# Routing a mixture of experts in groups of four tiles, and its expert loop written out

## The reference

```python
gu = x @ shared_gate_up_w
shared = _silu(gu[:, :Is]) * gu[:, Is:] @ shared_down_w
shared = shared * jax.nn.sigmoid(x @ shared_gate_w)
probs = jax.nn.softmax((x @ gate_w), axis=-1)
w, idx = jax.lax.top_k(probs, TOP_K)             # TOP_K = 8
w = w / jnp.sum(w, axis=-1, keepdims=True)
pos = ...   # how many earlier rows chose this expert
slot = jnp.minimum(pos, CAPACITY)                # CAPACITY = 128
buf = jnp.zeros((E, CAPACITY + 1, H)).at[e_flat, slot].set(x[tok])
act = _silu(gu_e[..., :I]) * gu_e[..., I:]       # gu_e = buf @ expert_gate_up_w
y = (act @ expert_down_w)[e_flat, slot] * w_flat[:, None]
y = jnp.where((pos < CAPACITY)[:, None], y, 0)
```

## Time and profile before

| | us |
|---|---|
| median of 3 runs (2916.77 to 2929.06) | 2918.77 |
| profiled execution | 2919.06 |
| its span | 2917.2 |
| `route` in it, first part | 1559.6 to 1652.3 |
| `route`, second part | 1652.3 to 1752.5 |
| `experts` | 1753.9 to 1889.3 |

### The profile page before, as it was taken

How to read it: one execution, slowest core, us unless ns; L and a number is a source line. 1 busy time by engine, 2 the same in 40 slices (tenths; PEclk the granted TensorE clock), 3 DMA queues, 4 the chain that set the end, 5 groups by cost and what they waited for, 6 DMA issues and landing times. The chain is left out here.

```text
span 2917.2 us, 69083 instructions
## 1 busy us (share of the span) xinstructions
PE 2553.8 (88%) x24287; PEld 1964.5 (67%) x24301; DVE 1767.3 (61%) x4144; ACT 1308.0 (45%) x3086; POOL 1479.7 (51%) x1701
## 2 busy tenths in 40 slices
PE   5875999999999999997785697859999999997996
PEld 2434878787878787785564455647888888885664
DVE  5654757575757576774565682346666665653663
ACT  3542646464646464653441223325444445442431
POOL 5774757475757475764661125456554445322320
PEclk9997999999999999998995699979999999999996
DMA  4331111111111111110002407553333334210000
GB/s 146 121 126 51 46 35 45 28 45 36 45 28 44 33 45 31 41 33 10 24 4 88 122 0 256 181 167 109 93 84 81 71 85 97 64 41 14 4 4 30
DMA packets 219788, 189.90 MB, mean 65 GB/s; under 512 B 86433, under 2 KB 206899, under 8 KB 219491
## 3 DMA queue, kind: packets, MB, share of 16 engines
q1 hardware_dynamic: 203378, 150.88, 17.4%
q0 software_dynamic: 10624, 30.99, 4.4%
q10 hardware_dynamic: 5488, 3.94, 0.5%
HBM read 151.42 MB, written 34.31 MB: 64 GB/s over the span
## 5 line engine op out<-in xcount | busy, mean ns | idle before, releaser
L840 POOL TENSOR_TENSOR rk<-ss,neg_half 128x32 f32<-128x32 f32 x64 | 347.5, 5430 | 212.1 <-DVE ss L746 212.1
L940 ACT ACTIVATE score<-score,ntop 128x289 f32<-128x289 f32 x256 | 135.4, 530 | 257.7 <-DVE ntop L757 254.9
L1024 PE MATMUL banks<-x_hi,wk_hi 128*128 128x256 f32 x1024 | 219.2, 297 | 32.0 <-DVE kT L740 31.2
L1544 PE MATMUL banks<-rowsT,qk 128*128 128x257 f32 x1024 | 243.1, 380 | 0.9 <-ACT qk L1471 0.9
L1024 PE MATMUL banks<-x_hi,wk_lo 128*128 128x256 f32 x1024 | 211.1, 289 | 0.0
L1024 PE MATMUL banks<-x_lo,wk_hi 128*128 128x256 f32 x1024 | 210.3, 288 | 0.0
L740 DVE COPY kT<-banks 128x512 f32<-128x512 f32 x256 | 176.0, 688 | 52.5 <-PE banks L1024 50.3
L1544 PEld LDWEIGHTS banks<-rowsT,qk 128*128 128x128 f32 x1024 | 189.2, 190 | 27.4 <-ACT qk L1471 1.2
L918 ACT ACTIVATE ksq<-kT 128x512 f32<-128x512 f32 x256 | 161.2, 630 | 85.1 <-DVE kT L740 83.1
L1024 PEld LDWEIGHTS banks<-x_hi,wk_hi 128*128 128x128 f32 x1024 | 163.5, 196 | 35.5 <-DVE kT L740 25.8
L754 DVE CUSTOM_DVE_ANT_0 score<-banks,rkb 128x289 f32<-128x289 f32 x256 | 108.7, 457 | 120.4 <-PE banks L1075 73.6
(11 more groups left out here) (364 smaller groups left out, 6799.0 us busy)
## 6 DMA issues: line engine op xcount, KB each, us to landing
rowsT<-in_ctxT SPq DMA_DIRECT2D x64, 257.0 KB, 2.8
raw<-in_ctx SPq DMA_DIRECT2D x64, 256.0 KB, 2.7
wgu<-in_expert_gu SPq DMA_DIRECT2D x64, 256.0 KB, 3.3
rows<-in_ctx SPq DMA_DIRECT2D x64, 256.0 KB, 3.1
scratch_qT<-qT SPq DMA_DIRECT2D x16, 512.0 KB, 2.6
scratch_kT<-kT SPq DMA_DIRECT2D x16, 512.0 KB, 3.2
q<-scratch_qT SPq DMA_DIRECT2D x64, 128.0 KB
kT<-scratch_kT SPq DMA_DIRECT2D x64, 128.0 KB
```

The source lines that it names most:

```text
L840: nc.gpsimd.tensor_tensor(m.rk[:], m.ss[:], kit.neg_half[:, 0:KF * H], ALU.pow).then_inc(s.rk, 1)
L940: nc.scalar.activation(m.score[:, c, :], m.score[:, c, :], ACT.Exp, bias=m.ntop[:, c:c + 1], accum_out=m.mass[:, c:c + 1]).then_inc(s.p, 1)
L1024: mm = nc.tensor.matmul(key_bank[i % 2][:, a * ROWS:(a + 1) * ROWS], w[:, f, pr * P:(pr + 1) * P], x[:, k, f, :], start=(at == 0), stop=(a ...
L1544: mm = nc.tensor.matmul(score[h][:, c - h * HALF, 0:CTX], m.qk[:, f, j, c * BT:(c + 1) * BT, :].rearrange("p h q -> p (h q)"), m.rowsT[:, ...
```

## The change

1. **Routing in groups of four tiles.** DVE runs over four tiles at once where it can (logit copy, `chosen`, `keep`, `place`, `key` are 256 columns); MAX8 and MATCH_REPLACE8 of the logits stay per tile. Eight normed tiles have buffers of their own, stored without weights (256 words). `before`, `ones` and `chosen` are bf16 (0 and 1 are exact), and the counting is done by matmuls over all earlier tiles' masks.
2. **Weights late.** Logits of all tiles are kept; shift, exponential, mask, sum and scale run once over 1024 columns, and one store in pieces of 64 words puts them beside the rows.
3. **Lists from two half lists.** Keys of rows 0 to 1023 go to partitions 0 to 63 and those of rows 1024 to 2047 to partitions 64 to 127, over 1024 columns. 16 rounds make both lists; the second half's slots are counted from the end, so that the reversing matrix `anti` and two matmuls add both lists into one.
4. **Shared network beside the routing.** Gate and up products are put between the routing steps on PE; POOL's copy of the transposed rows is gone, since ACT writes them in place.
5. **Experts written out.** No loops; the gather takes its numbers from `token` directly and waits for its ring slot. Weights are now the stationary side and the rows move, 128 columns, so that hidden rows come out transposed and their transpose and copy fall away. The routing weight is applied at the output. Fetches of the later experts' weights are spread over 56 of the 64 experts.

The core of the diff:

```diff
-                with sp.Fori(0, NT // 2) as u:
...
-                        sp.dma_start(d.routed_tiles[n], m.routed[:, k, :]).then_inc(stored[k], 16)
...
+                for n in range(NT):
+                    sp.wait_ge(s.xl, n + 1)
+                    sp.dma_start(d.routed_tiles[n][:, 0:D], m.rows[:, n % RT, :]).then_inc(stored[n % RT], 16)
+                    for e in range(n * (E_ // 2 // NT), (n + 1) * (E_ // 2 // NT)):
+                        early.load_one(sp, e, e, early.loaded)
+                sp.wait_ge(s.w, 1)
+                sp.dma_start(d.routed_tiles.rearrange("t p d -> p t d")[:, :, D:ROUTED], share).then_inc(s.weights_out, 16)
...
+                def largest(r):
+                    if r == 0:
+                        dve.wait_ge(s.ring, len(RING))
+                    else:
+                        dve.wait_ge(s.struck, r)
+                    nc.vector.max(m.order[:, 8 * r:8 * r + 8], m.keyT[:]).then_inc(s.order, 1)
...
+                for g, after in ((0, 5), (1, ROUNDS - 11)):
+                    for i in range(GT_):
+                        add(GT_ * g + i)
+                        if i % 2 == 0:
+                            strike(r)
+                            r += 1
+                        else:
+                            largest(r)
+                    for _ in range(after):
+                        strike(r)
+                        r += 1
+                        if r < ROUNDS:
+                            largest(r)
...
+                def inner(n, part):
...
+                    if n > 0:
+                        pe.wait_ge(s.gated if part == 0 else s.up, n)
...
+                for g in range(GN):
+                    for i in range(GT_):
+                        if g == 2 and i == 0:
+                            pe.wait_ge(s.order, ROUNDS)
+                            nc.tensor.transpose(kit.psum(2)[:, 0:P], m.order[:], kit.ident[:]).then_inc(s.order_ps, 1)
+                        if g == 2 and i == 2:
+
+                            pe.wait_ge(s.orderT, 1)
+                            nc.tensor.matmul(kit.psum(3)[:, 0:E_], kit.ident[:], m.orderT[:, 0:E_], start=True, stop=False)
+                            nc.tensor.matmul(kit.psum(3)[:, 0:E_], wm.anti[:], m.orderT[:, E_:2 * E_], start=False, stop=True).then_inc(s.list_ps, 1)
+                        outer(GT_ * g + i)
+                    for n in range(SN * (g + 2), min(SN * (g + 3), SN * GN)):
+                        inner(n, 0)
+                        inner(n, 1)
...
+        def due(e):
+
+            return [i for i in range(TURN) if (7 * i + 3) // 4 == e]
...
+                    for i in due(e):
+                        sp.wait_ge(s.y_ps, i + 1)
+                        weights.load_one(sp, TURN + i, i, late_in[i])
...
-                        nc.gpsimd.tensor_copy(m.index[:, b, :], kept.token[:, bass.ds(e, 1)]).then_inc(s.index, 1)
-                        hold(pool, s.index, e + 1, s.passed)
-                        nc.gpsimd.indirect_dma_start(m.rows[:, b, :], None, d.routed, bass.IndirectOffsetOnAxis(m.index[:, b, :], 0)).then_inc(rows_in[b], 16)
...
+                    if e >= EB:
+                        pool.wait_ge(s.out, e - EB + 1)
+                    nc.gpsimd.indirect_dma_start(m.rows[:, e % EB, :], None, d.routed, bass.IndirectOffsetOnAxis(kept.token[:, e:e + 1], 0)).then_inc(rows_in[e % EB], 16)
...
+                    for part in range(2):
+                        for f in range(FC):
+                            mm = nc.tensor.matmul(kit.psum(2 + e % 4)[:, part * CAP:(part + 1) * CAP], weights.wgu[:, e % TURN, f, part * I_:(part + 1) * I_], m.rowsT[:, e % 2, f, :],
+                                                  start=(f == 0), stop=(f == FC - 1))
                     mm.then_inc(s.gu_ps, 1)
...
+                for e in range(E_):
+                    if e + 2 < E_:
+                        rows_T(e + 2)
+                    if e + 1 < E_:
+                        products(e + 1)
+                    output(e)
```

More of the change, by code:

```diff
@@ L2387, in _, with group, rows @@
-                nc.vector.memset(m.count[:], 0.0).then_inc(s.c_set, 1)
+                def group(g):
+                    return slice(GT_ * g, GT_ * g + GT_)
+                def rows(first, count):
+                    if first >= RT:
+                        dve.wait_ge(s.ring_ps, RING["rows", (first + count - RT) // GT_ - 1, 1] + 1)
+                    for n in range(first, first + count):
+                        if n >= RT:
+                            dve.wait_ge(stored[n % RT], 16 * (n // RT))
+                        norm.rows(m.rows[:, n % RT, :], n).then_inc(s.xl, 1)
@@ L2388, in _ @@
                 norm.ready(dve)
+                nc.vector.memset(m.far_key[:], 0.0).then_inc(s.c_set, 1)
+                rows(0, 8)
                 dve.wait_ge(weights.loaded, weights.count)
[L2390 to L2434, removed]
@@ new lines, in logits @@
+                def logits(g):
+                    pe.wait_ge(s.ring, RING["rows", g, 1] + 1)
+                    if g > 0:
+                        pe.wait_ge(s.logit, g)
+                    for i in range(GT_):
+                        n = GT_ * g + i
+                        for f in range(FC):
+                            mm = nc.tensor.matmul(kit.psum(2)[:, i * (E_ + 1):(i + 1) * (E_ + 1)], m.xlT[:, f, n * P:(n + 1) * P], wm.wg[:, f, :], start=(f == 0), stop=(f == FC - 1))
+                    mm.then_inc(s.lg_ps, 1)
@@ new lines, in _ @@
+                inner(2, 0)
+                rows_T(3, 0)
+                rows_T(3, 1)
+                inner(2, 1)
+                logits(3)
+                places(2)
+                keys_T(1)
+                inner(3, 0)
+                inner(3, 1)
+                places(3)
+                keys_T(2)
+                inner(4, 0)
+                inner(4, 1)
+                keys_T(3)
+                for n in range(5, 8):
+                    inner(n, 0)
+                    inner(n, 1)
@@ new lines, in output @@
+                def output(e):
+                    dve.wait_ge(s.y_ps, e + 1)
+                    if e >= EB:
+                        dve.wait_ge(stored[e % EB], 16 * (e // EB))
+                    nc.vector.tensor_scalar(m.out[:, e % EB, :], kit.psum(6 + e % 2)[:, 0:D], m.rows[:, e % EB, D + e:D + e + 1], None, ALU.mult).then_inc(s.out, 1)
+                hidden(0)
+                for e in range(E_):
+                    if e + 1 < E_:
+                        hidden(e + 1)
+                    output(e)
@@ new lines, in output @@
+                def output(e):
+                    pe.wait_ge(s.hid, e + 1)
+                    if e >= 2:
+                        pe.wait_ge(s.out, e - 1)
+                    nc.tensor.matmul(kit.psum(6 + e % 2)[:, 0:D], m.hidT[:, e % 2, :], weights.wd[:, e % TURN, :], start=True, stop=True).then_inc(s.y_ps, 1)
+                rows_T(0)
+                rows_T(1)
+                products(0)
+                for e in range(E_):
+                    if e + 2 < E_:
+                        rows_T(e + 2)
+                    if e + 1 < E_:
+                        products(e + 1)
+                    output(e)
```

531 lines of the change are left out of this document (271 added, 260 removed).

## The result

| | us | ratio to before (95% interval) |
|---|---|---|
| kernel before, median of 4 runs | 2919.15 | |
| kernel after, median of 4 runs (2817.97 to 2826.43) | 2822.97 | 0.9668 (0.9642 to 0.9693) |
| forecast | 2816 (2800 to 2846) | |
| kernel after, unchanged, measured later on chip B (see the experiments) | 2803.86 | 0.9616 (0.9602 to 0.963) |

First the windows of the profile after, in the columns of the earlier trace rows: routing up to the first round, the rest of the routing block, both together, experts.

What follows compares the result with a forecast made beforehand. Bounds seen: a single-buffered PE-DVE ping-pong in routing, DVE's MAX8 and match rounds beside PE in the shared network, POOL's copy-wait-gather chain in the experts. 2919.1 - 81 (routing) - 22 (experts) = 2816 us, range 2800 to 2846.

Steps and rivals of the forecast that it cites:

- cold start, fill and small waits: Routing block: half clock at the start adds 4 to 5 us, fill 2, small waits, last residual add and close 4.
- rival 3: Routing part keeps its half clock of 0.50: costs 15 us, block 127 us, total 2831; chance 0.11.
- DVE's sum: Routing block: DVE's rounds, rows, choosing and placing, 1024-column operations and adds total 84 us, under PE's 101.
- Next to no slack: Routing block: DVE's lists and PE's work ahead of its wait both end at about 94 us; DVE lateness adds directly.
- 7.7 + 2.5 + 63 x 1.6 + 2: Expert block: start to first hidden product, cold clock, 63 steps of 1.6 us, 2 us more: 113 us against 135.4.
- The 0.06 us added to it for transfers: Expert step: taken as 1.6 us over PE's 1.54, with DMA beside it at 1.45 or 1.67 us.
- The other 2.5 us: Expert block's start: cold clock, its cost formerly hidden under POOL's pace, now adds 2.5 us.
- Rival 1: Experts: weight loads do not overlap products; step 2.18 us, block 150, total 2853, or 2835 with half; chance 0.08.
- The rule of the Trainium skill: Experts: 128-column matmuls paced at 81 ns instead of 56; eight records take 1.27 instead of 0.88 us, block 25 us more.
- Rival 2: Experts: transfers set the pace, gathers waiting behind fetches; step 1.9 to 2.0 us, block 135, total 2838; chance 0.09.
- Rival 4: Both blocks: PE held at clock 0.50; routing 207 us, experts 205, total 3003, slower than before; chance 0.02.
- The signs that were named: Also named for both blocks: list wait under 3 us, hidden products at 1.55 to 1.65 us, PE without long waits.

Runs made afterwards that it cites:

- the third run: The kernel after, unchanged, measured again on chip B: 2803.86 us, ratio 0.9616.
- the bunched fetches: Kernel after with the 32 late weights fetched one an expert over experts 0 to 31 instead of over 56 steps, chip B: 2807.05 us, ratio 0.963.
- the run on A: Kernel after with the index copy and its wait put back ahead of each gather, chip A: 2813.69 us, ratio 0.9648.
- two edits here: Kernel after with rings of three and one expert more of slack, 2805.5 us; kernel after without ACT's second wait, 2803.17 us; both on chip C.
- the four on A: Kernel after unchanged 2822.41 us; with keys of 1280 columns 2826.41; with first products behind the routing 2831.22; with index copy put back 2813.69.

## Why the prediction was right, and where it was off

**Routing block: forecast 112 us and -81, measured 111.4 and -83.** PE's work was put at 101 us plus 10 to 11 of cold start, fill and small waits; PE was busy 105.1 us with 6.3 us of pauses. (The 28.5 us for second products should have been 28.2 by the 0.22 us given; 28.3 was measured.) Busy time holds the slow records of the cold start, so the two splits agree. The clock was 0.85 up to the first round and full from there; rival 3, half clock to the end of the routing, didn't come. The kernel with the first products behind the routing shows that it was near: without the products among the steps the clock is 0.58 there.

**DVE under PE: right, with the slack a little too small.** MAX8 was forecast at 1.2 us and took 1.22, so its time goes by columns and not by partitions; DVE's sum was 77.0 us against 84. Last keys at 42 us (measured 42.2), all rounds done at 94 (the last match ends at 1650.1, 94.6 us in). "Next to no slack" was some 5 us, about 3 in DVE's waits between rounds and 1.6 in PE's work ahead of its wait.

**Experts: two terms were too large, and one effect was not foreseen.** Forecast was 7.7 + 2.5 + 63 x 1.6 + 2 = 113 us, bounds 107 and 121. Where nothing disturbs, the third run's trace has 7.7 + 63 x 1.552 + 1.6 = 107.0 us: 7.7 to the first multiply, then the steps, then the end. Most steps are PE's own count, 10 x 0.11 + 2 x 0.22 = 1.54 us. The 0.06 us added to it for transfers (1.45 to 1.67 us by two windows) made the forecast 3 us too long over 63 steps of 1.552, and transfers cost nothing: 335 GB/s moved beside a PE without a gap. The other 2.5 us were for the cold clock; the slow first steps cost some 0.4 us over the median step, on top of the 7.7. In the first measurement the block was 120.2 us, with late signals, which no row of before could show. The forecast of 2816 stands between the two levels, 2804 and 2823, and so it came near 2823 partly by luck: an error of 6 us one way and an unforeseen 19 us the other.

**Rival 1, weight loads pace the products, fell.** Eight records from 1730.29 to 1731.18 are 0.11 us each, as in the earlier trace rows. The rule of the Trainium skill, "TensorE: Matmul & The Clock Gate", "Back-to-back issue gap", which would have given 1.27 us for the eight, has no hold on these f32 records. **Rival 2, transfers, fell** with the bunched fetches. **Rival 4** fell with the clocks of 0.94 and 0.96.

**What POOL was bound by.** The prediction read 1.98 us as index copy, wait and gather. The pace was real, its cause was only half read: with copy and wait back, straight code does 1.45 us, below PE's step. So writing the loop out was enough to free POOL. Dropping the copy as well gained nothing that the run on A could show.

**The signs that were named.** Block of 108 to 116, PE over 85% busy, clock near 0.95, MAX8 at 1.2, no wait for the lists, gathers issued by waits for output: all there. A mean step of 1.55 to 1.65 us was there on B, at its lower end: 1.552, with most steps at 1.54 to 1.55. The first trace had 1.76, (1785.5 - 1674.6) / 63 between the first and last multiply.

## What to carry to other kernels

Count a written-out PE stream by start-to-start pace and trust the count: beside engines with cover it was met within 1%, and the margins added for transfers and for a cold start, 3 and 2.5 us, were the whole error. Before a cure for an unexplained stall is believed, run the unchanged kernel beside it on the same chip; two edits here seemed to gain 17 and 20 us and gained nothing. Look for work to put into the gaps of a serial choice, since it also keeps the clock up.

## What the runs showed of the hardware

Some of PE's semaphore updates were held for about 1.5 us and then came 40 to 90 ns apart, and what waited for them started late too: the silu at 1738.76 for products that ended at 1737.26. Between 1600 and 1800 us of the first trace 46 of 230 signalling matmuls were late and 74 had no record; all five traces with late updates (the first and the four on A) lack records, and the traces from chips B and C have no late one. That it is the chip, and not the time at which it was used, is not shown. The cause stays open. The missing records suggest that the recording of the updates has to do with it: the Trainium skill, "NOTIFIC — the notification-queue block", "7.1 Overflow: three behaviours, one of which stalls the engine", says that the block which writes such records can lose them or hold back the engine that makes them. If so, the 19 us would be the measurement's own. No run here could turn the recording off, so this is argued and not shown. The loops of before seem to escape it: their trace from the first measurement has no late update, with 27.5 updates of all kinds a us in the expert stage against 32.6 in the undisturbed trace of the kernel after, and their medians on A and B differ by 3.9 us only. That the rate decides is not shown either.

MAX8 took time by columns and not by partitions: 2.28 us at 64 x 2048, 1.22 at 128 x 1024, 1.49 at 128 x 1280 and 0.22 at 128 x 64.
